# Megakernel of a gated cross-attention block: another order for the attention's drain and the first FFN's front, two PSUM banks each for its gate and up products

## The reference, cut to what matters

```python
x = x + tanh(g_xattn[0]) * attention(layernorm(x), ctx)      # 16 heads of 16, int8-rounded q, k, v, uint8-rounded weights
x = x + tanh(g_ffn[0])   * moe(layernorm(x))                 # below
x = x + tanh(g_xattn[1]) * wkv(layernorm(x), ctx)
x = x + tanh(g_ffn[1])   * moe_2(layernorm(x))

# moe(h): x = w_norm * rmsnorm(h)
probs = softmax(x @ w_router)                # 32 experts
w_topk, sel = top_k(probs, 4)
# each expert takes at most its first 128 tokens, in token order
y[e] = (silu(rows[e] @ w_gate[e]) * (rows[e] @ w_up[e])) @ w_down[e]        # 256 -> 176 -> 256
out = sum over the 4 chosen of w_topk * y
sh = sigmoid(x @ w_shared_gate) * ((silu(x @ sw_gate) * (x @ sw_up)) @ sw_down)   # 256 -> 704 -> 256
return h + out + sh
```

## Time and profile before

| | before |
|---|---|
| median of 3 runs | 1166.4 us (1164.74 to 1167.02) |
| the profiled execution | 1166.14 us, of which the span is 1164.4 us |
| busy share of the span: PE, DVE, ACT, POOL | 90%, 82%, 77%, 60% |
| mean granted clock of TensorE | 0.994 of full |
| end of the loop over score blocks | about 700 us |
| last tile finished (L416) | 733.4 us |
| table of rows ready (L1479) | 777.85 us |
| first expert's turn (L1571) | 790.5 us |

### The profile page before, as it was taken

How to read it: one execution, slowest core, us unless ns; L and a number is a source line. 1 busy time by engine, 2 the same in 40 slices (tenths; PEclk the granted TensorE clock), 3 DMA queues, 4 the chain that set the end, 5 groups by cost and what they waited for, 6 DMA issues and landing times.

```text
span 1164.4 us, 24047 instructions
## 1 busy us (share of the span) xinstructions
PE 1048.7 (90%) x8281; PEld 606.3 (52%) x8396; DVE 950.6 (82%) x1748; ACT 891.8 (77%) x1546; POOL 701.3 (60%) x625
## 2 busy tenths in 40 slices
PE   8988888888888888888888889899998999999997
PEld 4743444444444444444444447656654465557775
DVE  6999999999999999999999996863336788953335
ACT  4779999999999999999999996734543576834441
POOL 3016888888777878888788776447651000753332
PEclk9999999999999999999999999899999999999999
DMA  6697998888888889888876764856938001523336
GB/s 193 120 163 149 173 172 162 169 169 171 167 172 175 165 166 170 178 162 170 155 118 111 115 109 78 243 170 181 321 115 331 0 1 46 178 84 109 97 97 233
DMA packets 388799, 176.36 MB, mean 151 GB/s; under 512 B 330413, under 2 KB 373650, under 8 KB 388680
## 3 DMA queue, kind: packets, MB, share of 16 engines
q1 hardware_dynamic: 381976, 157.85, 62.1%
q0 software_dynamic: 6480, 16.77, 4.3%
q10 hardware_dynamic: 224, 0.20, 0.1%
HBM read 52.70 MB, written 43.59 MB: 83 GB/s over the span
## 4 chain that ended last, share of the span: by engine, by line
PE 49%; DVE 28%; ACT 13%; issue 5%; DMA 2%; POOL 2%; SPq 1%; ACTq 0%; POOLq 0%; DVEq 0%
DVE top L426 22%; ACT weight L485 10%; PE bank L220 8%; PE bank L234 8%; PE bank L1187 4%; PE bank L2616 4%; PE bank L1580 3%; PE bank L252 3%; PE bank L2632 3%; PE bank L1166 2%; PE bank L1174 2%; PE bank L1853 1%; PE bank L1598 1%; PE bank L682 1%; POOL dispatched_rows L1823 1%
## 5 line engine op out<-in xcount | busy, mean ns | idle before, releaser
L485 ACT ACTIVATE weight<-bank,bias,sq_all 128x1024 uint8<-128x1024 f32 x512 | 609.9, 1201 | 24.0 <-PE bank L234 18.7
L426 DVE TENSOR_REDUCE top<-bank 128x1 f32<-128x512 f32 (+1 forms) x683 | 610.2, 951 | 11.5 <-PE bank L220 1.1
L537 POOL CAST weight<-turned 128x2048 bf16<-128x2048 uint8 x256 | 478.8, 1892 | 41.0 <-PE bank L252 22.2
L234 PE MATMUL bank<-kT,query 128*128 128x512 bf16 x917 | 284.1, 382 | 26.4 <-ACT weight L485 12.2
L252 PEld LDWEIGHTS bank<-v_sb,weight 128*128 128x128 bf16 x4096 | 172.0, 96 | 102.7 <-POOL weight L537 0.5
L220 PE MATMUL bank<-kT,qspace 64*128 64x512 bf16 x687 | 135.0, 387 | 55.8 <-DVE top L426 55.8
L252 PE MATMUL bank<-v_sb,weight 128*128 128x16 bf16 x4096 | 172.6, 170 | 0.8 <-POOL weight L537 0.4
L220 PE MATMUL bank<-kT,query 128*128 128x512 bf16 x329 | 124.8, 379 | 2.1 <-DVE top L426 1.4
L234 PEld LDWEIGHTS bank<-kT,query 128*128 128x128 bf16 x1024 | 59.9, 97 | 103.9 <-ACT weight L485 61.9
L1823 POOL DMA_INDIRECT dispatched_rows<-qspace,put x32 | 37.1, 1160 | 116.0 <-DVE qspace L2373 106.9
L485 ACT ACTIVATION_READ_ACCUMULATOR weight<-bank,bias,sq_all 128x1 f32 x512 | 101.7, 199 | 0.0
(11 more groups left out here) (352 smaller groups left out, 1471.7 us busy)
## 6 DMA issues: line engine op xcount, KB each, us to landing
dispatched_rows<-zeros SPq DMA_DIRECT2D x32, 524.0 KB, 3.1
answered_rows<-zeros SPq DMA_DIRECT2D x16, 512.0 KB, 3.2
late<-answered_rows SPq DMA_DIRECT2D x16, 512.0 KB, 6.3
erow<-dispatched_rows SPq DMA_DIRECT2D x39, 131.0 KB, 2.1
wgu<-in_L_ffn_w_gate SPq DMA_DIRECT2D x26, 176.0 KB, 3.8
wgu<-in_L_ffn_w_up SPq DMA_DIRECT2D x26, 176.0 KB, 3.7
query<-qspace SPq DMA_DIRECT2D x32, 128.0 KB, 3.1
turned<-weight SPq DMA_TRANSPOSE x256, 3.1
```

Source lines behind the costliest of these rows:

```text
L234: mm = pe.matmul(unit[u % 2][:, v * 512:(v + 1) * 512], query2[:, t % 2, h, :], kT[:, h // 2, first + v * 512:first + (v + 1) * 512], star ...
L426: ve.tensor_reduce(top[:, first:first + count], bank[:, first % 3:first % 3 + count, :], AX.X, ALU.max).then_inc(s_max, 1)
L485: ac.activation(weight8[:, n % BYTES, u * 1024:(u + 1) * 1024], unit[u], ACT.Exp, bias=bias[:, n:n + 1], scale=sq_all[:, n:n + 1], accum_o ...
L537: po.tensor_copy(weight[:, n % 3, :, :, :].rearrange("p c q two -> p (c q two)"), turned8[:, n % 3, :, :].rearrange("p c q -> p (c q)").bi ...
```

## The change

**Drain.** On TensorE the projections keep their sequence but stand elsewhere: turn 0, turn 1 and the two halves of group 0 go among the eleven units; turn 2, group 1's halves and group 2's come behind the last unit, with the remaining values summed between them up to a given head (`values_to`). Second halves of groups 1 and 2 go to bank 3. `router(0)` moves to the front. VectorE's `finish_tile` for the last tile and `offsets(1)` move into the drain's list, `add_projection` of group 1 is split around `normalise(0)`. ScalarE makes the deviations of group 0 after the last exponential.

**Banks.** The six gate products of group 0 alternate between banks 0 and 6, the up products between 1 and 4 (first two both in 1), so that a product needn't wait for the one just before it but for the one before that. Other groups keep banks 0 and 1.

**Front.** All four engines' lists are reordered; table switches of ScalarE's are fewer, since the exponentials of groups 2 and 3 stand together. `weigh` takes two groups at a time; the second call comes behind `take_table`. SP loads ten experts' weights in one run behind the shared weights, and then stores the rows: groups 0 and 1 after the first `weigh`, groups 2 and 3 after the second.

```diff
@@ attention_tensor @@
+                def values_to(head):
+                    nonlocal step
+                    step = sum_values(pe, step, NT * head - step, u)
...
                 turn_outputs(pe, 1, 0)
+                unit_and_values()
+                unit_and_values()
                 project_half(pe, 0, 0, 2)
+                unit_and_values()
                 unit_and_values()
                 unit_and_values()
                 pe.wait_ge(sm_["projections_added"], 1)
                 project_half(pe, 0, 1, 2)
+                while u < NUNIT:
+                    unit_and_values()
                 pe.wait_ge(sm_["outputs_copied"], 2)
                 turn_outputs(pe, 2, 0)
-                unit_and_values()
-                unit_and_values()
+                values_to(NHEAD - 3)
                 pe.wait_ge(sm_["projections_added"], 2)
                 project_half(pe, 1, 0, 2)
-                unit_and_values()
+                values_to(NHEAD - 2)
+                pe.wait_ge(s_exp, NUNIT)
+                project_half(pe, 1, 1, 3)
+                values_to(NHEAD)
                 pe.wait_ge(sm_["projections_added"], 3)
-                project_half(pe, 1, 1, 2)
-                unit_and_values()
+                project_half(pe, 2, 0, 2)
+                turn_rows(pe, 0)
                 pe.wait_ge(sm_["projections_added"], 4)
-                project_half(pe, 2, 0, 2)
-                unit_and_values()
-                while u < NUNIT:
-                    unit_and_values()
-                project_half(pe, 2, 1, 0)
-                step = sum_values(pe, step, -step % NT, u)
-                pe.wait_ge(s_exp, NUNIT)
-                turn_rows(pe, 0)
-                step = sum_values(pe, step, NT * (NHEAD - 1) - step, u)
-                pe.wait_ge(s_wr, 32)
-                pe.wait_ge(sm_["projections_added"], 5)
-                router(pe, 0)
-                step = sum_values(pe, step, NT, u)
+                project_half(pe, 2, 1, 3)
@@ attention_vector @@
                 add_projection(ve, 0, (2, 2))
+                group_statistics(ve, 0)
                 copy_outputs(2)
-                group_statistics(ve, 0)
-                add_projection(ve, 1, (2, 2))
+                add_projection(ve, 1, (2, 3), (0,))
                 normalise(ve, 0)
-                add_projection(ve, 2, (2, 0), (0,))
+                add_projection(ve, 1, (2, 3), (1,))
                 group_statistics(ve, 1)
-                add_projection(ve, 2, (2, 0), (1,))
+                finish_tile(ve, NT - 1)
+                add_projection(ve, 2, (2, 3), (0,))
+                offsets(ve, 1)
+                add_projection(ve, 2, (2, 3), (1,))
                 group_statistics(ve, 2)
@@ shared products @@
+            def gate_bank(n):
+                return 6 if n < NW0 and n % 2 else 0
+
+            def up_bank(n):
+                return 4 if n in range(2, NW0, 2) else 1
...
-                pe.wait_ge(sm_["gates_passed"], n)
+                if n == 1:
+                    pe.wait_ge(sm_["projections_added"], 2 * NG - 1)
+                elif n > 0:
+                    pe.wait_ge(sm_["gates_passed"], n - 1 if i == 0 else n)
...
-                pe.wait_ge(sm_["hidden_ready"], n)
+                if n == 2:
+                    pe.wait_ge(sm_["rows_copied"], NG)
+                elif n > 0:
+                    pe.wait_ge(sm_["hidden_ready"], n - 1 if i == 0 and n > 1 else n)
@@ front_sync @@
-                for e in range(3):
+                for e in range(OWN):
                     load_expert(sp, e)
                 for g in range(NG):
-                    sp.wait_ge(sm_["destinations_ready"], g + 1)
+                    sp.wait_ge(sm_["destinations_ready"], g // 2 + 1)
                     sp.dma_start(kept[...], rows0[...]).then_inc(s_kept, 16)
-                    for e in range(3 + 2 * g, min(5 + 2 * g, OWN)):
-                        load_expert(sp, e)
```

More of the change, by code:

```diff
@@ L1300, in fill_table, with gate0, up0 @@
                     mm.then_inc(sm_["table_products"], 1)
-                def hidden0(i, c0, c1):
-                    for c in range(c0, c1):
-                        shared_gate_tensor(pe, i, i, c)
-                        shared_up_tensor(pe, i, i, c)
+                def gate0(c):
+                    shared_gate_tensor(pe, 0, 0, c)
+                def up0(c):
+                    shared_up_tensor(pe, 0, 0, c)
                 def answers0(i):
                     shared_answers_tensor(pe, i, i)
+                pe.wait_ge(s_ofree, NT)
+                pe.wait_ge(sm_["outputs_copied"], 3)
+                turn_outputs(pe, 3, 0)
+                pe.wait_ge(s_wr, 32)
+                pe.wait_ge(sm_["projections_added"], 5)
+                router(pe, 0)
+                project_half(pe, 3, 0, 6)
+                project_half(pe, 3, 1, 7)
                 turn_rows(pe, 1)
+                pe.wait_ge(sm_["projections_added"], 6)
                 places(0)
-                pe.wait_ge(s_ofree, NT)
-                pe.wait_ge(sm_["projections_added"], 6)
-                turn_outputs(pe, 3, 0)
                 router(pe, 1)
                 turn_rows(pe, 2)
-                project_half(pe, 3, 0, 6)
-                project_half(pe, 3, 1, 7)
-                places(1)
-                router(pe, 2)
-                pe.wait_ge(s_wf, 64)
-                hidden0(0, 0, 1)
-                fill_table(0)
-                hidden0(0, 1, 2)
-                turn_rows(pe, 3)
-                places(2)
-                router(pe, 3)
-                hidden0(0, 2, 3)
+                pe.wait_ge(s_wf, 64)
+                gate0(0)
+                up0(0)
+                router(pe, 2)
+                gate0(1)
+                places(1)
+                turn_rows(pe, 3)
+                up0(1)
+                router(pe, 3)
+                gate0(2)
+                places(2)
+                up0(2)
+                fill_table(0)
+                gate0(3)
+                up0(3)
                 places(3)
-                hidden0(0, 3, 4)
                 fill_table(1)
-                hidden0(0, 4, 5)
+                gate0(4)
+                up0(4)
+                gate0(5)
                 fill_table(2)
-                hidden0(0, 5, 6)
+                up0(5)
                 fill_table(3)
@@ L1462, in weigh @@
                     settle()
[L1463 removed]
+                    ve.tensor_tensor(rows0[:, s, EPAY[2]:EPAY[3]], powers[:, :, E0:E0 + K0], share[:, s].unsqueeze(2).broadcast_to([P, s.stop - s.start, K0]),
                                      ALU.mult).then_inc(sm_["destinations_ready"], 1)
@@ L1485, in answers0 @@
                     shared_answers_vector(ve, i, i)
-                offsets(ve, 1)
                 choose(0)
-                finish_tile(ve, NT - 1)
-                ve.wait_ge(s_ofree, NT)
                 offsets(ve, 2)
-                take_slots(0)
-                weigh(0)
-                mark_slots(0)
-                choose(1)
                 add_projection(ve, 3, (6, 7))
                 group_statistics(ve, 3)
-                take_slots(1)
+                choose(1)
                 offsets(ve, 3)
-                weigh(1)
+                take_slots(0)
                 hidden0(0, 0, 1)
                 choose(2)
+                take_slots(1)
+                mark_slots(0)
+                choose(3)
                 hidden0(0, 1, 2)
                 take_slots(2)
-                weigh(2)
-                choose(3)
+                mark_slots(1)
                 hidden0(0, 2, 3)
                 take_slots(3)
-                settle()
-                mark_slots(1)
+                mark_slots(2)
                 hidden0(0, 3, 4)
-                mark_slots(2)
-                weigh(3)
+                weigh(0, 2)
                 hidden0(0, 4, 5)
@@ L1517, in front_vector @@
                 take_table()
+                weigh(2, 4)
                 answers0(0)
```

60 lines of the change are left out of this document (30 added, 30 removed).

## The result

The kernel after takes 1160.34 us (median of 6 runs, 1159.06 to 1160.88), the kernel before 1166.38 beside it (6 runs): ratio 0.9949, 95% interval 0.9939 to 0.9959, so 6.0 us faster. The profiled executions differ by 7.1 (1166.14 and 1159.07) and their spans by 7.0 (1164.4 and 1157.4); what follows is told on these two traces. The trace of the kernel after is one of its two fastest runs (1159.06 and 1159.07, the other four took 1160.24 to 1160.88), so it shows some 1 us more of gain than the medians do.

What follows compares the result with a forecast made beforehand. Bound: mostly VectorE's chain from choose(0) to the table, then the experts. Start 3.8 us later, 4.8 of work and 2.6 of waits won: table 3.6 earlier, less 0.5 for stores, 3.1 gained: 1163.3 us, range 1160.0 to 1168.0.

Steps and rivals of the forecast that it cites:

- Part 1: The drain: last exponential and last tile come earlier, but VectorE work moves behind them; choose(0) at 733.1, 3.8 us later.
- Part 3: Stores behind the table: second store pair puts the first gather at T + 7.8; cost 0 to 1.2 us, 0.5 taken.
- T: Time on the trace's clock when the table is ready: 777.85 before, forecast 774.3, 3.6 us earlier.
- two-sided bound on VectorE's stall: Drain: normalise(0) takes 3.5 to 3.9 us, stalled beside the last widening; without the stall TensorE would still set the pace.
- Part 2: VectorE from choose(0) to the table: work falls from 44.5 to 39.7 us, waits from 4.1 to 1.5.
- Sum 44.5 us in a stretch of 48.55, so about 4.1 us of waiting: VectorE from choose(0) to the table, kernel before: summed step prices 44.5 us, the rest about 4.1 us of waits.
- low stretch of the clock: Front: one stretch of TensorE at 1.2 GHz costs 1.8 us, partly absorbed by 0.7 spare; +1.0 us of waits.
- GpSimd's numbering: Front: group 3 numbered at 770, before mark_slots(3) ends (771 to 772); hidden, with 1 to 2 us to spare.
- Neither this nor the gathers behind it should reach the end: Experts' stage: GpSimd's scatters 6.8 us late against 10.4 us spare, so no cost at the end.
- Fewer waits yet: Front without a low clock stretch, stores hidden: gain 4.6 us, 5.5 with tighter VectorE joins, 1161; chance 0.12.
- The waits stay: Front: clock falls as often as now and 4.1 us of waits remain; T = 776.9, 1165.9; chance 0.20.
- Rows too late: Behind the table: second store lands late and delays the experts, 1167.2 to 1171; chance 0.20, 0.13 of it slower.

Runs made afterwards that it cites:

- light: Kernel before with three matmuls of 512 fp32 columns, results unused, in TensorE's pauses in the front: 1167.02 us, ratio 1.0009.
- the nine profiles: Profiled kernels with the same instructions from the drain to 737 us (three_fill one matmul more); TensorE's clock at 737 to 742: five at 1.00, four at 0.66 to 0.70.
- one_bank: Kernel after with gate products in bank 0 and up products in bank 1 only, every order kept: 1169.21 us, ratio 1.0026.
- three_again: Unchanged repeat of three_one, beside a repeat of the kernel after (1159.98 us) on one chip: 1159.85 us.
- all_behind: Kernel after with all four groups weighed in one call behind the table and all four stores behind it: 1165.46 us, ratio 0.9997.
- one half alone: Kernel before with the drain's lists of the kernel after; front, banks and weigh as before: 1169.8 us, ratio 1.0034.
- the other alone: Kernel after with the drain of the kernel before: 1164.55 us, ratio 0.9986.
- three_one: Kernel after with groups 0 to 2 weighed and stored ahead of the table and group 3 alone behind it: 1159.92 us, ratio 0.9947.
- three_fill: three_one with one more matmul of 512 fp32 columns, result unused, in TensorE's pause before places(0): 1162.22 us, beside 1159.85 of three_again.
- staged: Kernel after with three experts' weights loaded up front and two more behind each group's store, as before the change: 1173.37 us, ratio 1.0062.

## Why the prediction was right, and where it was off

The forecast was 1163.3 with a range of 1160.0 to 1168.0; it came to 1160.34, only 0.34 inside the range and below the case's own range of 1161.5 to 1164.5. The side and most of the mechanism were right, the gain (3.1) was half of what it is. The large errors all went the same way. Two small pairs cancelled by luck: a wait and an overlap in Part 1, and in Part 3 the 0.5 us charged to the first expert, which did not come, against 0.7 lost later, which was put at nothing. On the trace's own clock, term by term:

| term of the prediction | forecast | measured |
|---|---|---|
| last exponential | 716.9 | 716.60 |
| `finish_tile(15)` done | 728.3 | 726.97 |
| turn 3 ends | 729.65 | 728.88 |
| `choose(0)` starts | 733.1 | 732.08 |
| VectorE's work to the table | 39.7 | 37.6 |
| its waits | 1.5 | 0.6 |
| T | 774.3 | 770.28 |
| first gather | T + 7.8 | T + 7.9 |
| cost at the first expert | 0.5 | 0.0 |
| lost later in the experts' stage | 0 | 0.7 |

(37.6 is the stretch from 732.08 to 770.28, 38.2, less 0.6 of waits.)

**Part 1** held in its order and in its price: `choose(0)` later than before, not earlier, by 2.8 us for 3.8. Of the 1.0 too much, 0.8 was there when turn 3 ended and 0.2 is ScalarE's three steps. The 0.8 is a last unit that came 0.5 us sooner (it ended at 715.9 for 716.4) and a list behind it of 13.0 us for 13.2. That the list came out so near is the luck named above: TensorE waited 1.0 us in it for the last widening, which "if it doesn't wait" had left out, and its matmuls overlapped by 1.2 us more than the 0.3 taken. The two-sided bound on VectorE's stall was needed: `normalise(0)` took 3.4 us (720.25 to 723.66; 2.95 of it beside a widening of 1.96), less than the 3.5 to 3.9 taken, and it changed nothing: the last tile was finished 0.9 us before TensorE wanted it.

**Part 2** is where the sum was mis-sized, by 3.0 of the 4.0 us in T. The step that failed is "Sum 44.5 us in a stretch of 48.55, so about 4.1 us of waiting". It took the waits that the earlier trace rows shows for `hT` alone. The full list of VectorE's waits in that stretch (729.3 to 777.9) of the kernel before has three lines more:

```profile
DVE qspace L1445 <- PE bank L1288: 0.7, 1, 0.7
DVE tile_f L1477 <- PE bank L1298: 0.3, 1, 0.3
DVE qspace L1419 <- ACT qspace L1353: 0.2, 1, 0.2
```

The last of them lies just ahead of `choose(0)`. That makes 5.4 in the stretch, so its work was 43.15 us and not 44.5. My prices were single occurrences with the last instruction's own duration in them, and in the kernel after, start to start, the steps are shorter: `choose` 3.40 for 3.5, `take_slots` 1.32 for 1.44, `weigh` of two groups 1.36 for 1.6. The change took 5.55 us of work out (4.8 forecast) and 4.8 of waits (2.6 forecast). Some of these waits were the clock's: with the old order and a full clock from 740 to 778 the table came 1.4 us sooner in light, and no run separates the two further. The new waits were put between 0.5 and 4.1 and 1.5 was taken; 0.6 is at the low bound, because the low stretch of the clock for which I had added 1.0 did not come in this execution. By the nine profiles it comes in about half of them and then makes the table up to 1 us later, so the term fitted about half of the executions and not the profiled one.

The banks do what Part 2 says: no wait for an up product is left, and one_bank gives 8.9 us back, part of it with a lower clock.

**GpSimd's numbering** was hidden, as costed. Its last one in the kernel after, beside the third mark:

```profile
761.70 4.20 POOL L1285 TENSOR_SCALAR late<-qspace 128x128 bf16<-128x128 f32 x4
```

```profile
762.02 2.28 DVE L1496 TENSOR_TENSOR late<-slot_b,qspace 128x2048 bf16<-128x2048 bf16 x1
```

4.20 us where the earlier trace rows has 2.35 for it alone, so 1.85 more beside a mark of 2.28. It ended at 767.6, ahead of `mark_slots(3)`. By the Trainium skill (SBUF — State Buffer, Who interferes with whom), under which the two would not run at the same time, it would be 2.35 + 2.28 = 4.63, an estimate; the trace nearly agrees.

**Part 3.** The new wait had the size it was given: weigh 1.36 for 1.6, the second issue 0.4 behind the first, 5.25 us from issue to landing for 4.7. It cost the first expert nothing. By the Trainium skill's knee (SBUF — State Buffer, The DMA setup-cost knee) the pair was an estimate of 4.5; 5.25 was measured, so it is low by 0.75 here. What failed is "Neither this nor the gathers behind it should reach the end". I had set the 6.8 us that GpSimd starts late against 10.4 us of spare over the whole stage. But part of this spare lies behind the last gather, where it can help no gather, and the ones that it used to issue ahead now stand in the stage: by the second row of the windows 79.5 - 57.84 - 58 x 0.3 = 4.3 us are left. The last gather held TensorE for 0.5 us. The prediction named this among what would make it wrong; three_again shows its size, 0.8 us, and that removing it gains nothing measurable.

**The rivals.** *Fewer waits yet* (1161, given 0.12) is nearest to what came: no low stretch, tighter joins, `choose(0)` 1 us sooner. *The waits stay* did not come; one_bank shows what they would have cost. *Rows too late* did not come either, but all_behind shows how near it is: a first gather 4 us later after the table costs 5.1.

## What to carry to other kernels

When a stretch is costed as work plus waits, take the whole list of the engine's waits and subtract it from the stretch; a sum of single durations over-counts the work, and the error passes straight into what the new order is said to gain. Parts of a reordering are not additive: here one half alone loses 3.6 us, the other alone gains 1.65, both gain 6.0, because a list that is in order passes on whatever comes late. And when a queue is given work later than before, count its spare only up to the last item that somebody waits for.

## What the runs showed of the hardware

Nearly the same instructions ran at 1.00 or at 0.66 to 0.70 of TensorE's clock over the same 5 us (737 to 742) in different executions, five profiles to four; one unchanged kernel did both (0.66 in three_one, 1.00 in three_again). A stretch at 0.51 occurred with TensorE busy 7.00 of 7.00 us (light), and filling the longer of the two pauses ahead of a fall did not prevent it (three_fill). In staged one load's issue on SP's queue took from 0.43 to 2.00 us, and the last store, due at 773.1, was issued at 784.5 behind the loads ahead of it. In the kernel after, the second of two stores issued 0.4 us apart landed 5.25 us after its issue. The last of four landed 7.0 us after its own in all_behind.
